# From the 20th tile on, NF4 codes stored and spread as bytes, in a ring of four tiles that is filled three tiles ahead

## The reference, cut to what matters

```
x = x + masked_linear(norm(x))            # 512 x 512, mask by 32 x 32 blocks
x = x + int4_linear(norm(x))              # 512 x 512, packed int4
x = x + nf4_block(norm(x))                # below
x = x + fp4_mlp(norm(x))                  # gate/up 1376 x 512, down 512 x 1376, NVFP4 quantised

# nf4_block: every weight is dequantised from int32 codes 0 to 15
W = NF4[codes] * scales (one scale per 64 codes);  lin(x) = x W^T + (x A^T) B^T   (LoRA, rank 16)
attn = (q + k + v) / 3;  x1 = x + out(attn)          # four 512 x 512 weights
h = silu(gate(x1)) * up(x1);  x1 + down(h)           # gate, up 1792 x 512, down 512 x 1792
```

## Time and profile before

| what | value |
|---|---|
| median of 3 runs | 782.47 us (779.07 to 785.65) |
| the profiled execution, its own time | 782.3 us |
| its span, first to last instruction | 780.7 us |
| PE busy / DVE busy / ACT busy / POOL busy | 90% / 70% / 57% / 28% |
| mean granted TensorE clock | 0.969 of 2.4 GHz |
| moved by DMA | 110.78 MB |

### The profile page before, as it was taken

The page is one execution under the profiler, slowest core; times in us unless marked ns, Lnnn a source line. Parts: engine busy times, 40 slices in busy tenths (PEclk is TensorE's granted clock), DMA queues, the critical chain, the costliest instruction groups (busy, mean ns, idle before and its releaser), DMA issues.

```text
span 780.7 us, 10709 instructions
## 1 busy us (share of the span) xinstructions
PE 703.8 (90%) x3830; PEld 528.6 (68%) x3830; DVE 545.1 (70%) x1017; ACT 448.0 (57%) x582; POOL 219.7 (28%) x208
## 2 busy tenths in 40 slices
PE   2799866797999989999998999997999999989998
PEld 1566533575777756677675777775777789967886
DVE  6889886656577677878798976587543534487883
ACT  3767778476778596887886712374332111245552
POOL 1004100003355547557578554220401000000000
PEclk9999977898999999999999999999999999989999
DMA  9646588887457677686875301210301111100001
GB/s 339 191 142 210 159 248 252 258 283 223 175 164 242 190 244 251 210 258 204 263 220 185 122 28 37 69 52 18 107 28 38 30 35 36 56 1 13 28 28 40
DMA packets 55540, 110.78 MB, mean 142 GB/s; under 512 B 9904, under 2 KB 20560, under 8 KB 55232
## 3 DMA queue, kind: packets, MB, share of 16 engines
q1 hardware_dynamic: 42912, 80.28, 32.7%
q0 software_dynamic: 4384, 14.09, 6.2%
q10 hardware_dynamic: 8192, 15.73, 6.0%
HBM read 92.19 MB, written 17.89 MB: 141 GB/s over the span
## 4 chain that ended last, share of the span: by engine, by line
PE 56%; DVE 16%; ACT 8%; DMA 8%; issue 7%; SPq 4%; ACTq 0%; POOL 0%; DVEq 0%; POOLq 0%
PE bank L1287 15%; PE bank L1288 14%; PE bank L1289 14%; DMA rep<-codes 4%; ACT hot L1709 3%; PE bank L1401 2%; DVE hot L1958 2%; DMA wide_buf<-in_down_flat 2%; DVE x L2071 1%; PE bank L1596 1%; PE bank L1443 1%; ACT c L1666 1%; DVE bank L1984 1%; PE bank L1547 1%; DVE q_a L2034 1%
## 5 line engine op out<-in xcount | busy, mean ns | idle before, releaser
L1709 ACT ACTIVATE hot<-rep,levels 128x2048 f16<-128x2048 f16 x94 | 192.9, 2092 | 25.6 <-DMA rep<-codes 15.4
L1287 PE MATMUL bank<-zt_h,w_h 128*128 128x512 f32 (+1 forms) x232 | 93.5, 403 | 2.5 <-DVE zt_l L2059 2.0
L1288 PE MATMUL bank<-zt_l,w_h 128*128 128x512 f32 (+1 forms) x232 | 91.6, 395 | 0.0
L1289 PE MATMUL bank<-zt_h,w_l 128*128 128x512 f32 (+1 forms) x232 | 91.5, 394 | 0.0
L1287 PE MATMUL bank<-w_h,xq_h 128*128 128x512 f32 (+1 forms) x192 | 73.9, 385 | 2.3 <-ACT xq_l L1803 2.1
L1289 PE MATMUL bank<-w_h,xq_l 128*128 128x512 f32 (+1 forms) x192 | 71.7, 373 | 0.0
L1288 PE MATMUL bank<-w_l,xq_h 128*128 128x512 f32 (+1 forms) x192 | 71.7, 373 | 0.0
L1401 PE MATMUL bank<-hot,diag 128*32 128x512 f16 x856 | 60.6, 394 | 8.6 <-ACT hot L1709 8.2
L1958 DVE TENSOR_SCALAR hot<-rep,levels 128x2048 f16<-128x2048 f16 x56 | 52.7, 941 | 7.1 <-DMA rep<-codes 7.0
L1996 DVE TENSOR_TENSOR w_l<-bank,w_h 128x512 fp32r<-128x512 f32 x46 | 31.7, 689 | 35.9 <-ACT w_h L1717 35.6
L2214 POOL TENSOR_TENSOR q_a<-q_a,q_m 128x384 f32<-128x384 f32 (+3 forms) x34 | 35.9, 1055 | 65.6 <-DVE q_m L1845 65.5
(11 more groups left out here) (215 smaller groups left out, 1666.2 us busy)
## 6 DMA issues: line engine op xcount, KB each, us to landing
rep<-codes SPq DMA_DIRECT2D x56, 512.0 KB, 4.8
codes<-c SPq DMA_DIRECT2D x28, 256.0 KB, 3.6
raw<-in_codes_gu_t ACTq DMA_DIRECT2D x14, 512.0 KB, 5.7
sc<-in_scales_gu_t SPq DMA_DIRECT2D x56, 128.0 KB, 3.9
raw<-in_codes_attn_t ACTq DMA_DIRECT2D x7, 512.0 KB, 5.0
raw<-in_codes_down_t ACTq DMA_DIRECT2D x7, 512.0 KB, 5.8
sc<-in_scales_down_t SPq DMA_DIRECT2D x28, 128.0 KB, 3.1
wide_buf<-in_gate_flat SPq DMA_DIRECT2D x5, 512.0 KB, 4.7
```

What stands on the lines that cost most here:

```text
L1287: PE.matmul(psum, lh, rh, start=first, stop=False, **kw)
L1288: PE.matmul(psum, lh, rl, start=False, stop=False, **kw)
L1289: return PE.matmul(psum, ll, rh, start=False, stop=last, **kw)
L1709: S.activation(hots[plan.slot[hot_ring(t), (t, m)]][:], codes_in_place(t), ACT.Relu, bias=levels[:, at:at + 1], scale=levels[:, at + 1:at ...
```

## The change

From tile 20 on (`act_falls`) a code is one byte instead of two. The cast writes int8 into the first half of `c16`, the ship goes to one of four new byte rooms, and the spread moves 2 KB instead of 4 KB to each partition. `rep0` and `rep1` then hold two tiles each, so four tiles fit (t % 4), and the spread of tile t waits for the readers of tile t - 4 instead of t - 2 (`rep_before`; on the way over, tiles 20 to 23, for 18 and 19). The spread is added three tiles ahead instead of two; at the turn of tile 18 those of tiles 20 and 21 stand together. The hit and both ramps read int8 and write fp16 as before. For all jobs, those before tile 20 too, the ship stands half a turn earlier: in the second half of the even turn, ahead of the scales.

```diff
+def rep_before(t):
+    if t < ACT_FALLS:
+        return t - 2
+    return t - 4 if t >= ACT_FALLS + 4 else ACT_FALLS - 2 + (t - ACT_FALLS) // 2
...
-            p.sends(f"rep_in{t % 2}", ("rep", t))
+            p.sends(f"bytes_in{t % 4}" if act_falls(t) else f"rep_in{t % 2}", ("rep", t))
...
-            if u == 1 and i + 2 < len(jobs):
-                ship(i + 2)
-            spread(t + 2)
+            if t + 2 <= ACT_FALLS:
+                spread(t + 2)
+            if t + 3 > ACT_FALLS:
+                spread(t + 3)
...
             yield
+            if u == 0 and i + 2 < len(jobs):
+                ship(i + 2)
             if t < tiles:
                 assemble(t)
                 scales(t + 3)
...
+    byte_rooms = [nc.dram_tensor(f"codes8_{i}", [CU, P, 512], I8).ap() for i in range(4)]
...
-        return reps[t % 2][:] if t >= CU else first_codes[t][:]
+        if t < CU:
+            return first_codes[t][:]
+        return codes_bytes(t) if act_falls(t) else reps[t % 2][:]
+
+    def codes_bytes(t):
+        half = t % 2 * 1024
+        both = reps[t % 4 // 2][:].rearrange("p j n -> p (j n)")
+        return both[:, half:half + 1024].bitcast(I8).rearrange("p (j n) -> p j n", j=4)
+
+    def cast_to(i):
+        both = c16[:].rearrange("p u n -> p (u n)")
+        return both[:, 0:512].bitcast(I8).rearrange("p (u n) -> p u n", u=CU) if act_falls(CU * i) else c16[:]
...
-                S.copy(c16[:], raw[:]).then_inc(sem("cast_act"), 1)
+                S.copy(cast_to(i), raw[:]).then_inc(sem("cast_act"), 1)
...
-                    sp.wait_ge(*done("dve", "hit", t - 2, HITS if act_falls(t - 2) else FALLS))
-                    sp.wait_ge(*done("act", "ramp", t - 2, RISES))
-                src = rooms[t // CU % 4][t % CU].rearrange("(r j) n -> r (j n)", j=4)
-                SP.dma_start(reps[t % 2][:], src.unsqueeze(1).broadcast_to([32, 4, 4 * 512])).then_inc(
+                    last = rep_before(t)
+                    sp.wait_ge(*done("dve", "hit", last, HITS if act_falls(last) else FALLS))
+                    sp.wait_ge(*done("act", "ramp", last, RISES))
+                src = room_of(t // CU)[t % CU].rearrange("(r j) n -> r (j n)", j=4)
+                SP.dma_start(codes_in_place(t), src.unsqueeze(1).broadcast_to([32, 4, 4 * 512])).then_inc(
```

More of the change, by code:

```diff
@@ L1248, in codes_in_place, with room_of @@
     def codes_in_place(t):
-        return reps[t % 2][:] if t >= CU else first_codes[t][:]
+        if t < CU:
[8 more added lines that the diff above has]
+        return both[:, 0:512].bitcast(I8).rearrange("p (u n) -> p u n", u=CU) if act_falls(CU * i) else c16[:]
+    def room_of(i):
+        return byte_rooms[i % 4] if act_falls(CU * i) else rooms[i % 4]
     def raw_codes(t):
@@ L2335, in sp_program @@
                     sp.wait_ge(*landed(("rep", CU * (i - 4) + CU - 1)))
-                SP.dma_start(rooms[i % 4].rearrange("u p n -> p u n"), c16[:]).then_inc(dma_sem(("codes", i)), 16)
+                SP.dma_start(room_of(i).rearrange("u p n -> p u n"), cast_to(i)).then_inc(dma_sem(("codes", i)), 16)
             elif kind == "spread":
```

## The result

| | before | after |
|---|---|---|
| median of ten runs each, same chip | 780.69 us (776.23 to 785.65) | 787.16 us (784.53 to 790.19) |
| ratio, 95% interval | | 1.0086 (1.0057 to 1.0115) |
| profiled execution, its span | 782.3 us, 780.7 us | 787.0 us, 785.7 us |

The change costs 6.7 us (0.0086 of 780.7), with 4.5 and 9.0 as the ends of the interval. The forecast was 784.0 against 782.3, a cost of 1.7 us, with a range up to 797: the sign holds, and the cost is 5 us larger.

The account below looks back on a forecast made before the run. PE was taken to set the pace, with 15.1 us of idle time to win back. From 782.3 us, 5.2 of gains off and 6.9 for the hit on gave 784.0 us; range 772 to 797, its own 777 to 790.

Parts of the forecast that it names:

- The hit: On DVE, a byte hit takes 1.336 us, 0.53 more; 13 hits in the chain of waits cost 6.9 us (0 to 20.1).
- The gains: Sum of the four savings from spreads, a store, the ship's place and traffic: 5.2 us less.
- Spreads one tile earlier and half as long: No ramp or hit from tile 21 on waits for a spread; PE's gaps at 287 and 382 us go: 2.2 us.
- Less traffic: Smaller spreads and ships move 12.4 MB less of 110.8, speeding a load at 171 us: 0.8 us (0 to 2.5).
- That store: Store that DVE awaits 2.6 us, ahead of PE's 1.59 us gap at 304.05 us, comes earlier: 1.2 us (0 to 1.6).
- The ship ahead of the scales: Earlier ship no longer delays a spread, as at 129.32 us before tile 20: 1.0 us gained (0 to 3.7).
- New waits on the SP queue: Ship waits for the cast, a job's first spread at most 2 to 3 us for its ship; counted as nothing.
- What would show it: Signs in the profile after: hit, ramp and spread times, spread waits, DVE share, PE gaps; PE idle between 5 and 20 us.
- A: In the stage, spreads set the pace of ramps and hits everywhere, so 11.4 us of PE idle go: 770 us, chance 0.18.
- B: In the stage's dense stretches DVE's queue becomes the bound, each hit's 0.53 us passed on: 797 us, chance 0.17.
- C: On DVE the hit reads bytes one at a time, 61 us more DVE work: about 805 us, chance 0.06.
- D: All was hidden: neither the gains nor the longer hits reach PE: 782 us, chance 0.09.

Follow-up runs that it names:

- its half hit: The change, but from tile 20 on (tile 26 excepted) the hit covers 1024 of its 2048 codes, so weights are wrong: 777.22 us, ratio 0.9958.
- bytes two ahead: Kernel before with int8 codes, two buffers, spreads two tiles ahead, ship in its old place: 786.51 us; with the hit over 1024 of 2048 codes 774.30 us.
- the fp16 kernel with the ship late: Kernel before with a third buffer and spreads three ahead from tile 26, fp16 codes, ship in its old place: 786.12 us, ratio 1.0094.
- the change with the hit first: The change, but from tile 20 on the next tile's hit and ramps stand ahead of the low part that waits for `w_h`: 779.35 us, ratio 1.0004.
- fp16 with the ship early: Kernel before with a third buffer and spreads three ahead from tile 26, fp16 codes, ship moved ahead of the scales: 777.27 us, ratio 0.9961.
- the byte kernel with two tiles of lead and the hit first: Kernel before with int8 codes, two buffers, spreads two ahead, ship moved ahead of the scales, hit ahead of the low part: 778.77 us, ratio 0.9993.

## Why the prediction was right, and where its sizes were off

**The hit, +6.9 us: 10.0 and 10.5 us measured.** The mechanism is the one named: the step behind the hit on DVE's queue is later, and PE sees about half of it. The term was under-sized. The working took 0.53 us for each of 13 hits in the chain of waits. Between the change and its half hit a hit differs by 0.52 us (1.59 against 1.07), as taken, so 10.0 us is the growth of 19 hits, not 13. Against the kernel before a hit is 0.59 us longer (1.59 against 1.00), and its part of the chain has grown from 13.0 to 22.3 us (9.1% of 245), by 9.3 us. What was too small is mainly the share of the growth that reaches PE. Each single price is known to about 3.4 us, which all but reaches 6.9; it is the two together, 10.0 and 10.5, that speak against it. How the excess divides isn't settled. One part is seen at 304 us, by way of the store; two further costs are seen but not priced: POOL's longer steps (below) and the clock behind the gaps.

The place was predicted less well. I wrote that 0.53 us disappears where DVE waits for `w_h` "right ahead of the hit". An idle time ahead of an instruction doesn't hide its growth, since the instruction starts at its end; only idle time behind it does. The hit put ahead of that wait recovers 6.4 of the 10 us, so part of the cost was there; how large a part is not shown, since fp16 hits gained 2.3 and 1.4 us by the same move. This is the sentence that failed.

**The gains, -5.2 us: -3.3 (0.9 to 5.7) measured** with the change's own arrangement, -5.5 with bytes two ahead. The size is within the error, but the reasons were put on the wrong part. "Spreads one tile earlier and half as long" was priced at 2.2 us for the lead: with bytes the lead adds nothing that can be measured (+6.7 against +4.9; with half the hit -3.3 against -5.5), in fp16 1.5 us, within the error. "Less traffic" was priced at 0.8 us by a place at 171 us, where PE idles for 2.50 us at 180.10 us before; that gap is missing too from the fp16 kernel with the ship late, which is the same up to there, so it comes and goes with the execution. The real work of the bytes is in the stage: they alone, two tiles ahead, take the waits for spreads from 14.8 to 1.9 us, and with half the hit the kernel gains 5.5. I had put that down to the extra turn, and wrote that my sum did not need the shrinking.

The Trainium skill ("DMA: Bandwidth & Descriptors", Anatomy of one DMA), read as a fixed time plus bytes, gave an estimate of 0.6 us for a halved spread. In the change with the hit first the median from issue to landing is 4.0 us for 256 KB and 5.3 us for the 512 KB of the tiles before 20, beside other traffic; before, it was 4.8 us over all 56. So a spread shrank by 0.8 to 1.3 us, somewhat more than the estimate:

```profile
rep<-codes SPq DMA_DIRECT2D x38, 256.0 KB, 4.0
rep<-codes SPq DMA_DIRECT2D x18, 512.0 KB, 5.3
```

**That store, -1.2 us: nothing in the change.** DVE's wait for the store of `gate_dq` is 3.0 us (2.6 before), and the gap of 1.59 us at 304.05 us stands at 303.75. The store was late since a hit and an assembly were, as I wrote, but the longer byte hit keeps them late. With half the hit and in fp16 with the ship early the wait is 0.8 to 1.1 us and that gap is gone, so the term is real only while the hit is short; in the working gains and cost were priced apart.

**The ship ahead of the scales, -1.0 us.** Alone -1.6 (-4.1 to +0.9): not told from nothing. Its true part is another: without it the lead costs 10.3 us more in fp16; with bytes 3.1 us more, within the error.

**New waits on the SP queue, nothing.** In the change the first spreads wait 11.5 us for ships, five times, the longest 4.3 us; I had written at most 2 to 3. Whether they cost something is argued, not shown: bytes two ahead with half the hit is 2.2 us ahead of the change with half the hit, inside the error. But "it pays on that queue, not on PE" is wrong as a rule: in the kernel with the late ship the same wait went on to a store, to DVE and into 10.3 us of the kernel's time.

**What would show it.** Seen: byte hits of 1.34 us, ramps of 2.09, no wait for a spread, DVE at 89%, the gaps of 287 and 382 us gone, that at 330 us longer (1.82 for 1.53), those around 420 us together longer (1.25, 0.34 and 1.59 for 0.89 and 1.58), and PE's idle time of 12.9 us between the two bounds of 5 and 20. Seen only in part: spreads of 256 KB landing "well under 4.8" us. The profile after has no time for them; in the two byte kernels with the hit first the median is 4.0 us. In the byte kernel with two tiles of lead and the hit first, two late ones stand in the chain of waits (start, us):

```profile
332.69 5.66 DMA rep<-codes
...
363.62 6.92 DMA rep<-codes
```

These are picked for being late, as the 6.57 and 9.35 us of the earlier trace rows are.

**The rivals.** *A* (the spreads set the pace, 770 us) has the waits right, which all go, but with the hit's cost taken out the gain is 3.3 to 5.5 us, not 12. *B* (DVE's queue becomes the bound) is the mechanism of the result at half its price: 0.45 to 0.55 us pass on for each of DVE's, not one. *C* (bytes read singly) falls by 1.34 us a hit. *D* (all hidden) falls by the two half-hit kernels, 10 us away from their sisters. The clock of 0.90 in *A* is that of 415 to 425 us, with the gaps in it; from 422 to 432 us, right behind them, it is 0.83.

## What to carry to other kernels

Idle time of an engine covers a longer instruction only if it lies behind it in that engine's order, and before anything that another engine awaits; idle time ahead of it covers nothing. So before an instruction is made longer, look at what stands in front of it, and move it ahead of the wait if it needs nothing from there. When a transfer is late, try it smaller and earlier apart from each other: here either one took nearly all the waits away, and the type that made it smaller cost more on DVE than both gave. A transfer that is moved earlier on a queue must take its producer's transfer with it, or the whole queue stands behind the pair.

## What the runs showed of the hardware that was not expected

- DVE's `tensor_scalar` on 128 x 2048 int8 takes 1.337 us, to the nanosecond almost what int32 takes (1.336), against 0.805 for fp16. 1024 int8 columns take 0.819, so each 1024 columns add 0.52 us. A source a quarter as wide as int32 is not read faster; 2-byte codes are the fast ones. ACT takes 2.09 us for all three. The Trainium skill ("VectorE: DVE Perf Modes", What auto-detection actually checks) keeps the fastest mode for operands that are all of 16 bits, and the trace agrees.
- Longer hits slow POOL. Over the whole kernel the same 208 POOL steps take 219.70 us before and 219.84 us with half the hit, but 233.46 us in the change and 234.22 us in bytes two ahead. The longer fp16 hit in three short pieces does not do it: 213.46 us. In one place of the change, DVE and POOL in the timeline:

```profile
426.68 2.90 DVE L1984 TENSOR_SCALAR hot<-rep,levels 128x2048 f16<-128x2048 int8 x1
```

```profile
427.18 1.32 POOL L2240 TENSOR_TENSOR q_a<-q_a,q_m 128x512 f32<-128x512 f32 x1
428.57 2.17 POOL L2243 TENSOR_TENSOR q_a<-q_a,q_m 128x512 f32<-128x512 f32 x1
```

  The hit's 1.34 us become 2.90, longer by 1.56, about the POOL step beside it (1.32), the twin of the earlier trace rows; POOL's next step, begun 1.0 us before the hit ends, takes 2.17 us, where the same step at 418.83 us took 1.30 (mean of this form 1.52). The Trainium skill ("SBUF — State Buffer", Who interferes with whom) has the one engine wait for the other's whole instruction at a shared pair of ports, when DVE is in a two-port mode. The lengths agree with it. It also gives the pair to the engine that issues first; by the recorded starts the hit began 0.50 us ahead of the POOL step, here and in the earlier trace rows, and is yet the one that got longer, which no run explains.
- One fp16 hit cut in three (512, 512 and 1024 columns) took 1.88 us instead of 1.00 us. A piece of 512 columns, 0.40 us at the least, takes 0.675 us on the mean, hardly less than one of 1024 (0.690):

```profile
L1960 DVE TENSOR_SCALAR hot<-rep,levels 128x512 f16<-128x512 f16 x76 | 48.2, 675 | 2.3 <-DMA rep<-codes 2.2
L1960 DVE TENSOR_SCALAR hot<-rep,levels 128x1024 f16<-128x1024 f16 x38 | 26.2, 690 | 0.0
```
